# One block of feed-forward, state-space scan and feed-forward on one core: the order of work comes from tables, and TensorE adds matmuls of zeros to y in steps 2, 31 and 39

## The chip, the cores and the metric

The kernel runs on one core of one Trainium2 chip. The metric is device time in microseconds (us) of one execution; the median of 3 runs of the kernel before is 5074.88 us.

## What is computed

The input x is (4, 2048, 512), all float32. Three sub-blocks are added to x in turn; each takes a layer norm (no weights) of what it is given.

```python
# feed-forward (twice, factor 0.5): token mix with the token before, then
r = sigmoid(xr @ W_r.T);  k = square(relu(xk @ W_k.T));  out = r * (k @ W_v.T)
# state-space block (once), E = 1024 channels, N = 16 states
xz = layernorm(x, ln_w, ln_b) @ W_in.T;  xs, z = split(xz)
xc = silu(b_conv + causal_conv4(xs));  dt, B, C = split(xc @ W_xproj.T)
delta = softplus(dt @ W_dt.T + b_dt)
h_t = exp(delta_t * A) * h_(t-1) + delta_t * B_t * xc_t     # for all 1024 x 16 states
y_t = sum_n h_t * C_t + D_skip * xc_t
out = (y * silu(z)) @ W_out.T + x
```

## The kernel before

The 8192 tokens are worked on in 16 **chunks** of 512 tokens, the four batches in turn. A chunk has 64 **steps**: 4 quarters of the channels (256 channels, two tiles of 128) by 16 states. In step s, for the state s % 16 of the quarter s // 16:

- ScalarE (ACT) makes `decay` = exp(delta * A), in two instructions and a one-column copy between them (`make_decay`, L837 to L840), into one of two buffers. It has first to save the last column of the buffer's old content (`save`, L846), which waits for the step before the last to be done.
- GpSimd (POOL) makes `dbx` = u * B (`product`, L1255, and a one-column sum, L1259), up to four steps ahead.
- VectorE (DVE) runs the scan in place (`scan`, L1037, 128x1024) and multiplies by C (`weigh`, L1045) into `g`, of which there are two.
- TensorE (PE) adds g to the accumulator `y_acc` in PSUM by eight 128x128 transposes (`sum_g`, L510), one step later.
- SyncE loads B and C of the next steps, spread over 128 partitions.

Everything else is put between these, at fixed steps of the same loop: feed-forward 0 and the first half of the state-space block of the chunk in front (`front`, chunk it+1), the gate and output of this one, and the output projection and feed-forward 1 of the chunk behind (`back`, it-1). Each engine has its own program, in which every piece of work stands in an `if ... s == ...` after the step's own work, so the place in the program and the order of the `if`s fix what is queued behind what. Engines wait for each other by semaphores, whose counts follow from the order of names in a `Marks` list. An engine can run a step or so ahead of another: the decay of step s is made while DVE scans step s-1.

The pieces that matter here: `ffn_norm` (L642) writes the normalized rows of feed-forward 1 over `rows[1]`, so it waits until `res_scratch<-rows` (L336), the store of the residual that `make_res` (L731) wrote there, has landed. `keep_y` (L819) copies y_acc to SBUF at a quarter's end; the first `sum_g` of the next quarter waits for it. `turn_y` (L522) transposes it, DVE multiplies it with the gate (`gate_y`, L1014). `z` (L462) and `xs` (L452) are the two halves of the input projection, each piece of four 128x512 matmuls (eight records); `gate_tanh` (L826) and `gate_silu` (L1008) take z, `conv_start` (L753), `conv_taps` (L997), `conv_tanh` (L762) and `conv_silu` (L1003) take xs. `dt_proj` (L486) and `softplus` (L788, with a table load before and one after, L796) make delta of a quarter. `xproj` (L474), eight matmuls in steps 49 and 50, and `x_rows` (L771) make dt, B and C of the chunk in front. `ffn_turn` is at L401, `ffn_add` at L1244. All outputs of PE but y_acc go through the two banks of `mm`; `GROUPS` lists them in PE's order with their bank, and `bank_free` makes PE wait until the last content of the bank was read.

Of the kernel before, what the change touches and what calls it, by code (L numbers as in the profile page):

```python
# [5 lines left out]
ALU = mybir.AluOpType  # L6
# [4 lines left out]
P = 128  # L11
# [22 lines left out]
def build(nc, x, mu_r, mu_k, w_r, w_k, w_v, ln_w, ln_b, w_in, w_conv, b_conv, w_x, w_dt, b_dt,  # L34
# [20 lines left out]
    with ExitStack() as ctx:  # L55
# [6 lines left out]
        def sem(name):  # L62
# [45 lines left out]
        zero = sb("zero", [P, 1])  # L108
# [27 lines left out]

        newton = ["guess"] + [f"{q}{i}" for i in range(NEWTON) for q in ("yy", "vyy", "half", "y")]
        f_pe = [Marks(sem("ffn0_pe"), "T0 T1 T2 T3 k0 k1 k2 k3 r0 r1 r2 r3 v0 v1 v2 v3"),
                Marks(sem("ffn1_pe"), "T0 T1 T2 T3 r0 r1 r2 r3 k0 k1 k2 k3 v0 v1 v2 v3")]
        f_act = [Marks(sem("ffn0_act"), "ln0 ln1 ln2 ln3 xn0 xn1 xn2 xn3 lead last pk0 pk1 pk2 pk3 "  # L140
                       "pr0 pr1 pr2 pr3 rel0 sq0 rel1 sq1 rel2 sq2 rel3 sq3 th0 th1 th2 th3"),
                 Marks(sem("ffn1_act"), "ln0 ln1 ln2 ln3 xn0 xn1 xn2 xn3 lead last pr0 pr1 pr2 pr3 "
                       "pk0 pk1 pk2 pk3 th0 th1 th2 th3 rel0 sq0 rel1 sq1 rel2 sq2 rel3 sq3")]
        f_dve = [Marks(sem("ffn0_dve"), "st0 st1 st2 st3 mv0 mv1 mv2 mv3 xk0 xk1 xk2 xk3 xr0 xr1 xr2 xr3 "
                       "g0 g1 g2 g3"),
                 Marks(sem("ffn1_dve"), "st0 st1 st2 st3 mv0 mv1 mv2 mv3 xr0 xr1 xr2 xr3 xk0 xk1 xk2 xk3 "
                       "g0 g1 g2 g3")]
# [22 lines left out]
        y_pe = Marks(sem("y_pe"), "T0 T1 T2 T3 T4 T5 T6 T7 o0 o1 o2 o3")  # L170
        y_dve = Marks(sem("y_dve"), "g0 g1 g2 g3 g4 g5 g6 g7 x0 x1 x2 x3")


        GROUPS = [("f0T0", 1, f_act[0], "xn0", 1), ("f0T1", 1, f_act[0], "xn1", 0),
                  ("f0T2", 1, f_act[0], "xn2", 1), ("f0T3", 1, f_act[0], "xn3", 0),
                  ("YT6", -1, y_dve, "g6", 1), ("YT7", -1, y_dve, "g7", 0), ("dt1_0", 0, h_act, "xa1", 1),
                  ("dt1_1", 0, h_act, "xb1", 0), ("o0", -1, y_dve, "x0", 0), ("f0k0", 1, f_act[0], "rel0", 1),
                  ("f0k1", 1, f_act[0], "rel1", 0), ("f0k2", 1, f_act[0], "rel2", 1),
                  ("f0k3", 1, f_act[0], "rel3", 0), ("f0r0", 1, f_act[0], "th0", 1),
                  ("f0r1", 1, f_act[0], "th1", 0), ("f0r2", 1, f_act[0], "th2", 1),  # L180
                  ("f0r3", 1, f_act[0], "th3", 0), ("f0v0", 1, f_dve[0], "g0", 1),
                  ("f0v1", 1, f_dve[0], "g1", 0), ("f0v2", 1, f_dve[0], "g2", 1),
                  ("f0v3", 1, f_dve[0], "g3", 0), ("dt2_0", 0, h_act, "xa2", 1), ("dt2_1", 0, h_act, "xb2", 0),
                  ("o1", -1, y_dve, "x1", 1), ("o2", -1, y_dve, "x2", 0), ("o3", -1, y_dve, "x3", 1),
                  ("mT0", 1, m_act, "xn0", 0), ("mT1", 1, m_act, "xn1", 1), ("mT2", 1, m_act, "xn2", 0),
                  ("mT3", 1, m_act, "xn3", 1), ("z0", 0, z_dve, "0", 0), ("xs0", 1, m_dve, "c2_0", 1),
                  ("z1", 0, z_dve, "1", 0), ("xs1", 1, m_dve, "c2_1", 1), ("YT0", 0, y_dve, "g0", 0),
                  ("YT1", 0, y_dve, "g1", 0), ("z2", 0, z_dve, "2", 1), ("dt3_0", 0, h_act, "xa3", 0),
                  ("dt3_1", 0, h_act, "xb3", 1), ("xs2", 1, m_dve, "c2_2", 0),
                  ("f1T0", -1, f_act[1], "xn0", 1), ("f1T1", -1, f_act[1], "xn1", 1),  # L190
                  ("f1T2", -1, f_act[1], "xn2", 1), ("f1T3", -1, f_act[1], "xn3", 1),
                  ("xs3", 1, m_dve, "c2_3", 0), ("z3", 0, z_dve, "3", 1), ("xs4", 1, m_dve, "c2_4", 0),
                  ("YT2", 0, y_dve, "g2", 1), ("YT3", 0, y_dve, "g3", 1), ("xs5", 1, m_dve, "c2_5", 0),
                  ("f1r0", -1, f_act[1], "th0", 1), ("f1r1", -1, f_act[1], "th1", 1),
                  ("xs6", 1, m_dve, "c2_6", 0), ("f1r2", -1, f_act[1], "th2", 1),
                  ("f1r3", -1, f_act[1], "th3", 1), ("xs7", 1, m_dve, "c2_7", 0),
                  ("f1k0", -1, f_act[1], "rel0", 1), ("f1k1", -1, f_act[1], "rel1", 0),
                  ("xp", 1, m_act, "xp", 1), ("f1k2", -1, f_act[1], "rel2", 0),
                  ("f1k3", -1, f_act[1], "rel3", 1), ("dt0_0", 1, h_act, "xa0", 0),
                  ("dt0_1", 1, h_act, "xb0", 1), ("f1v0", -1, f_dve[1], "g0", 0),  # L200
                  ("f1v1", -1, f_dve[1], "g1", 1), ("f1v2", -1, f_dve[1], "g2", 0),
                  ("f1v3", -1, f_dve[1], "g3", 1), ("z4", 0, z_dve, "4", 0), ("z5", 0, z_dve, "5", 1),
                  ("z6", 0, z_dve, "6", 0), ("YT4", 0, y_dve, "g4", 1), ("YT5", 0, y_dve, "g5", 1),
                  ("z7", 0, z_dve, "7", 0)]
# [1118 lines left out]
```

## Time and profile before

| | us |
|---|---|
| median of 3 runs (lowest, highest) | 5074.88 (5071.17, 5075.77) |
| the profiled execution's own time | 5075.57 |
| its span, first to last instruction | 5073.8 |
| PE busy | 4318.3 (85%) |
| DVE busy | 4484.9 (88%) |
| ACT busy | 2897.2 (57%) |
| POOL busy | 3179.3 (63%) |

The profile is of one execution. Its views are: a page (busy times, and the span in 40 slices with TensorE's granted clock), the waits (who waited for whom in total), busy times in stretches of the span, and the timeline (instructions in order of time, merged; in brackets the idle time of the engine before one and what ended it). Matmul records overlap, since matmuls are pipelined.

### The profile page before, as it was taken

What the parts mean: (1) busy time and instruction counts of PE and PEld (TensorE: products, weight loads), DVE (VectorE), ACT (ScalarE), POOL (GpSimd) and SP (SyncE); (2) the same over time, 40 slices, a digit from 0 to 9 for tenths busy, and PEclk for the clock granted to TensorE, in tenths of its full rate; (3) what the DMA queues carried; (4) which work ended last, traced back from release to release, by engine and by line L of the source; (5) the groups of instructions that cost most, each with busy time, mean ns of one, the idle gap of its engine ahead of it and who ended that gap; (6) DMA issues with size and microseconds to landing.
All of it is one profiled execution on the core that took longest, in us unless ns stands there. A gap on an engine that the chain in (4) does not pass through costs nothing.

```text
span 5073.8 us, 57587 instructions
## 1 busy us (share of the span) xinstructions
PE 4318.3 (85%) x16640; PEld 2420.2 (48%) x16640; DVE 4484.9 (88%) x3650; ACT 2897.2 (57%) x6355; POOL 3179.3 (63%) x3328
## 2 busy tenths in 40 slices
PE   6778889898888989889898888989889898888777
PEld 2444445454454545445454454545445454454443
DVE  2799999899999999899899999999899899998982
ACT  3555656566565656656565655656656566565552
POOL 1666667576675756667576665756667576675761
PEclk9888999899999999999999999989999999999788
DMA  2445656465654656556565655656566565654651
GB/s 79 146 138 176 164 168 181 137 180 152 181 166 147 182 165 173 162 167 183 143 179 147 183 165 151 179 168 170 165 174 171 150 179 144 179 166 138 172 156 63
DMA packets 423052, 810.69 MB, mean 160 GB/s; under 512 B 41264, under 2 KB 41264, under 8 KB 418640
## 3 DMA queue, kind: packets, MB, share of 16 engines
q1 hardware_dynamic: 422736, 807.00, 55.4%
q8 instruction: 135, 2.21, 0.2%
q14 instruction: 181, 1.48, 0.1%
HBM read 772.25 MB, written 34.60 MB: 159 GB/s over the span
## 4 chain that ended last, share of the span: by engine, by line
PE 39%; DVE 24%; issue 12%; ACT 9%; POOL 8%; DMA 6%; SPq 0%; DVEq 0%; POOLq 0%; ACTq 0%
DVE decay L1037 10%; PE y_acc L510 9%; DVE g L1045 8%; PE mm L437 6%; POOL dbx L1255 5%; PE mm L415 5%; PE mm L426 5%; PE mm L462 4%; PE mm L452 4%; DMA res_scratch<-rows 3%; DMA c_all<-bc_scratch 3%; DVE xc L997 3%; PE mm L474 3%; PE mm L486 1%; DVE mix_k L974 1%
## 5 line engine op out<-in xcount | busy, mean ns | idle before, releaser
L1255 POOL TENSOR_TENSOR dbx<-u,b_all 128x1024 f32<-128x1024 f32 x1024 | 2413.3, 2357 | 1211.0 <-DVE g L1045 1207.9
L1037 DVE TENSOR_TENSOR_SCAN decay<-decay,state,dbx 128x1024 f32<-128x1024 f32 x1024 | 2405.9, 2350 | 261.2 <-ACT decay L840 253.4
L510 PE MATMUL y_acc<-ident,g 128*128 128x128 f32 x8192 | 1177.9, 291 | 541.3 <-DVE g L1045 472.1
L510 PEld LDWEIGHTS y_acc<-ident,g 128*128 128x128 f32 x8192 | 992.1, 149 | 1092.0 <-DVE g L1045 766.2
L1045 DVE TENSOR_TENSOR g<-decay,c_all 128x1024 f32<-128x1024 f32 x1024 | 1242.0, 1213 | 7.9 <-DMA c_all<-bc_scratch 0.9
L837 ACT ACTIVATE decay<-delta,neg_a 128x512 f32<-128x512 f32 x1024 | 708.6, 692 | 36.9
L840 ACT ACTIVATE decay<-delta,neg_a 128x511 f32<-128x511 f32 x1024 | 686.8, 671 | 0.0
L437 PE MATMUL mm<-wbuf_c,col 128*128 128x512 f32 x1024 | 460.8, 594 | 21.9 <-ACT delta L788 20.5
L846 ACT ACTIVATE state<-decay 128x2 f32<-128x2 f32 x1024 | 167.3, 163 | 454.8 <-DVE g L1045 453.8
L997 DVE SCALAR_TENSOR_TENSOR xc<-mm,conv_sb,xc 128x509 f32<-128x509 f32 (+2 forms) x384 | 285.1, 743 | 64.3 <-ACT xs_last L755 55.0
L1259 POOL TENSOR_TENSOR dbx<-dbx,carry 128x1 f32<-128x1 f32 x1024 | 247.1, 241 | 80.3
L437 PEld LDWEIGHTS mm<-wbuf_c,col 128*128 128x128 f32 x1024 | 185.1, 190 | 212.6 <-issue 210.4
L452 PE MATMUL mm<-xn_col,wbuf_a 128*128 128x512 f32 x512 | 257.8, 652 | 1.4 <-DVE xc L997 1.4
L753 ACT ACTIVATE xc<-mm,evec,conv_sb 128x512 f32<-128x512 f32 x128 | 99.2, 775 | 276.1 <-PE mm L452 241.9
L462 PE MATMUL mm<-xn_col,wbuf_c 128*128 128x512 f32 x512 | 254.9, 645 | 0.0
L707 ACT ACTIVATE col<-mm 128x512 f32<-128x512 f32 x128 | 76.8, 600 | 299.2 <-PE mm L415 299.2
L452 PE MATMUL mm<-xn_col,wbuf_d 128*128 128x512 f32 x512 | 239.8, 612 | 1.2 <-ACT xn_col L740 0.9
L415 PE MATMUL mm<-mix_k,wbuf_c 128*128 128x512 f32 x512 | 234.8, 603 | 4.4 <-DVE mix_k L974 4.4
L826 ACT ACTIVATE gate<-mm 128x512 f32<-128x512 f32 x128 | 76.2, 595 | 284.1 <-PE mm L462 284.0
L426 PE MATMUL mm<-wbuf_d,xin 128*128 128x512 f32 x512 | 233.4, 600 | 4.4 <-DVE xin L979 4.4
L533 PE MATMUL mm<-wbuf_a,gate 128*128 128x512 f32 x512 | 234.0, 600 | 2.1 <-DVE gate L1014 0.8
L462 PE MATMUL mm<-xn_col,wbuf_b 128*128 128x512 f32 x512 | 231.7, 595 | 0.0
(98 smaller groups left out, 5170.0 us busy)
## 6 DMA issues: line engine op xcount, KB each, us to landing
b_all<-bc_scratch SPq DMA_DIRECT2D x1024, 256.0 KB, 3.9
c_all<-bc_scratch SPq DMA_DIRECT2D x1024, 256.0 KB, 4.6
wbuf_d<-in_w_r SPq DMA_DIRECT2D x32, 1024.0 KB, 8.6
wbuf_c<-in_w_v SPq DMA_DIRECT2D x32, 1024.0 KB, 8.1
xin<-in_x SPq DMA_DIRECT2D x16, 1024.0 KB, 8.1
wbuf_c<-in_w_k SPq DMA_DIRECT2D x16, 1024.0 KB, 8.2
wbuf_d<-in_w_in SPq DMA_DIRECT2D x16, 1024.0 KB, 8.0
wbuf_a<-in_w_in SPq DMA_DIRECT2D x16, 1024.0 KB, 9.8
```

Of the source, the lines that this page charges most:

```text
L415: last = pe.matmul(bank(it, f"f{i}k{j}"), wk[:, ct, j * P:(j + 1) * P], mix_k[:, ct, :], start=ct == 0, stop=ct == CT - 1)
L426: last = pe.matmul(bank(it, f"f{i}r{tb}"), mix_r[:, ct, tb * P:(tb + 1) * P], wr[:, ct, :], start=ct == 0, stop=ct == CT - 1)
L437: last = pe.matmul(bank(it, f"f{i}v{tb}"), col[:, ct, tb * P:(tb + 1) * P], wv[:, ct, :], start=ct == 0, stop=ct == CT - 1)
L452: last = pe.matmul(bank(it, f"xs{e}"), win[:, ct, e % 4 * P:(e % 4 + 1) * P], xn_col[:, slot, ct, :], start=ct == 0, stop=ct == CT - 1)
L462: last = pe.matmul(bank(it, f"z{e}"), win[:, ct, e % 4 * P:(e % 4 + 1) * P], xn_col[:, slot, ct, :], start=ct == 0, stop=ct == CT - 1)
L510: last = pe.matmul(y_acc[:, tb, j * P:(j + 1) * P], g[:, s % PAIRS, j, tb * P:(tb + 1) * P], ident[:, :], start=n == 0 and j == 0 and tb % ...
L837: act.activation(d[:, 0, :], delta[:, q % 2, 0, :], ACT.Exp, scale=neg_a[:, e, n:n + 1]).then_inc(decay_done, 1)
L840: act.activation(d[:, 1, 1:W], delta[:, q % 2, 1, 1:W], ACT.Exp, scale=neg_a[:, e + 1, n:n + 1]).then_inc(decay_done, 1)
L997: dve.scalar_tensor_tensor(out=o, in0=src[:, 0:W - late], scalar=conv_sb[:, e, q:q + 1], in1=o, op0=ALU.mult, op1=ALU.add).then_inc(m_dve. ...
L1037: dve.tensor_tensor_scan(d, d, flat(dbx[:, s % DBX, :, :]), state[:, batch, s, 0:1], ALU.mult, ALU.add).then_inc(scan_done, 1)
L1045: dve.tensor_tensor(g[:, s % PAIRS, :, :], decay[:, s % PAIRS, :, :], c_all[:, s % CRING, :].unsqueeze(1).broadcast_to([P, QT, W]), ALU.mu ...
L1255: pool.tensor_tensor(dbx[:, s % DBX, :, :], u[:, q % 2, :, :], b_all[:, s % BRING, :].unsqueeze(1).broadcast_to([P, QT, W]), ALU.mult).the ...
```

## The change

The order is now written as tables of step numbers, one for each kind of work, and each engine's program asks the tables in one fixed order. A number below 0 or above 63 means the iteration before or after. Names in `Marks` lists and `GROUPS` are sorted from the tables. Of the tables two lines, with the new one:

```diff
-                    if back and 19 <= s < 25:
-                        out_proj(it, b, (s - 17) // 2, (s - 19) % 2)
+        OUT = ((4, 5), (19, 20), (21, 22), (23, 23))
...
+        RES = 25
...
+        ZEROS = {2: 2, 31: 2, 39: 2}
```

```diff
-        zero = sb("zero", [P, 1])
+        zero = sb("zero", [P, P])
...
-            pe.wait_ge(init_pool, 3)
+            pe.wait_ge(init_pool, 12)
...
+            def add_zeros(n):
+
+                for _ in range(n):
+                    pe.matmul(flat(y_acc[:, 0:2, :]), zero[:, :], ident[:, :].unsqueeze(1).broadcast_to([P, 4, P]),
+                              start=False, stop=False, skip_group_check=True)
...
+                    if scn and s in ZEROS:
+                        add_zeros(ZEROS[s])
...
-                    if front and s == 27:
-                        make_res(f)
-                    if back and s == 30:
-                        ffn_norm(1, b, front)
...
+                    if front and s == RES:
+                        make_res(f)
+                    if back and s == NORM[1]:
+                        ffn_norm(1, b, front)
```

`add_zeros` comes last in its step: two matmuls of a zero 128x128 tile with 512 columns, added to y_acc, so y does not change. It is called three times in each of the 16 chunks: 96 such matmuls in all.

The tables hold most numbers of before, but not all. Moved to another step:

- ACT: `make_res` 27 to 25; `skip_columns` of the four quarters 56, 12, 29, 41 to 58, 14, 31, 43; `ffn_before_r` of feed-forward 0 from 5, 6, 6, 6 to 6, 7, 7, 7.
- PE: the first `ffn_k` of feed-forward 0 from 6 to 5; the last part of `out_proj` 24 to 23.
- DVE: the third gate of feed-forward 0 from 17 to 18, the last `out_stats` 26 to 27, one `ffn_mix_r` of feed-forward 1 from 38 to 39.
- POOL: the four `ffn_add` of feed-forward 1 from 59, 60, 61, 62 to 57, 58, 59, 60.
- SyncE: the load of w_k for feed-forward 1 from 26 to 25, the second load of w_in 27 to 26, the store of the residual 28 to 26, the store of the output 63 to 61.

Four `mamba_turn` outputs and the third `ffn_turn` of feed-forward 1 (from bank 1 to bank 0) changed banks. And within a step the order of some pieces is another, on ACT, PE and DVE.

**ACT, steps 24 to 30** of a chunk, where the residual (`rows<-xin`, the second such row) and the norm of feed-forward 1 (`rows<-xout`) stand. Before, from after step 26's decay:

```order
L740 ACTIVATE xn_col<-mm,vec 128x512 x2
L846 ACTIVATE state<-decay 128x2
...
L740 ACTIVATE xn_col<-mm,vec 128x512 x2
L731 ACTIVATE rows<-xin,shift,rs 128x512 x4
...
L642 ACTIVATE rows<-xout,shift,rs 128x512 x4
L826 ACTIVATE gate<-mm 128x512
L762 ACTIVATE rows<-xc 128x512
```

Now, from step 25:

```order
L781 ACTIVATE rows<-xin,shift,rs 128x512 x4
L896 ACTIVATE state<-decay 128x2
...
L790 ACTIVATE xn_col<-mm,vec 128x512 x2
...
L876 ACTIVATE gate<-mm 128x512
L812 ACTIVATE rows<-xc 128x512
L692 ACTIVATE rows<-xout,shift,rs 128x512 x4
```

The residual is made before the columns of `mamba_columns`, not after them, and the gate's and the convolution's tanh now stand ahead of the norm.

**ACT, step 49**, `keep_y` of quarter 2 (`y_rows<-y_acc`) beside relu and square of feed-forward 1 (`col`). Before:

```order
L707 ACTIVATE col<-mm 128x512
L709 ACTIVATE col<-col 128x512
L819 ACTIVATE y_rows<-y_acc 128x512 x2
L846 ACTIVATE state<-decay 128x2
```

Now:

```order
L869 ACTIVATE y_rows<-y_acc 128x512 x2
L757 ACTIVATE col<-mm 128x512
L759 ACTIVATE col<-col 128x512
L896 ACTIVATE state<-decay 128x2
```

`keep_y` no longer stands behind the relu, which waits for four matmuls; in step 33 it moved ahead of the gate's tanh in the same way.

**PE, steps 31 to 33**: the transposes of y, the third z, the projection of dt for quarter 3. Before:

```order
L522 MATMUL mm<-ident,y_rows 128x128 x8
L510 MATMUL y_acc<-ident,g 128x128 x8
L462 MATMUL mm<-xn_col,wbuf_c 128x512 x4
L510 MATMUL y_acc<-ident,g 128x128 x8
L486 MATMUL mm<-xdbl,wdt_sb 128x512
L494 MATMUL y_acc<-ident,spare 128x128 x8
L486 MATMUL mm<-xdbl,wdt_sb 128x512
```

Now:

```order
L586 MATMUL mm<-ident,y_rows 128x128 x8
L576 MATMUL y_acc<-ident,zero 128x512 x2
L568 MATMUL y_acc<-ident,g 128x128 x8
L520 MATMUL mm<-xn_col,wbuf_c 128x512 x4
L568 MATMUL y_acc<-ident,g 128x128 x8
L544 MATMUL mm<-xdbl,wdt_sb 128x512 x2
L552 MATMUL y_acc<-ident,spare 128x128 x8
```

The zeros stand behind the transposes of y and ahead of `sum_g`, and both dt matmuls now come before the skip terms.

## Rows read from the trace of the kernel before

**Rows 1.** Span with the mean granted clock, and the page's clock in 40 slices.

```profile
core 0: 5073.8 us, clock 0.935
...
PEclk9888999899999999999999999989999999999788
```

**Rows 2.** The waits: who waited for whom, us in total, times, longest us.

```profile
ACT rows L642 <- DMA res_scratch<-rows: 56.9, 14, 5.2
...
DVE decay L1037 <- ACT decay L840: 253.4, 187, 20.1
...
ACT xdbl L771 <- PE mm L474: 126.2, 16, 8.1
```

**Rows 3.** Stretches: from:to length, busy PE, PEld, DVE, ACT, POOL, PEclk, DMA, GB/s.

```profile
3183.99:3487.75 303.76, 266.43 (x1040) 148.91 (x1040) 280.10 (x230) 180.64 (x397) 198.43 (x207) 0.95 0.58 166
3184.00:3193.10 9.10, 5.85 (x48) 5.18 (x48) 9.03 (x6) 8.35 (x21) 6.90 (x5) 1.00 0.75 242
3312.40:3337.90 25.50, 17.12 (x58) 10.42 (x59) 19.16 (x17) 12.81 (x28) 11.20 (x12) 0.73 0.46 133
```

**Rows 4.** Timeline, steps 27 to 30 (start, us, instruction, idle time before it).

```profile
3298.31 2.92 ACT L731 ACTIVATE rows<-xin,shift,rs 128x512 f32<-128x512 f32 x4
...
3303.95 0.38 SPq L336 DMA_DIRECT2D res_scratch<-rows  x1
...
3313.17 0.20 POOL L1227 TENSOR_TENSOR xc<-xc,head 128x3 f32<-128x3 f32 x1
...
3315.19 2.93 ACT L642 ACTIVATE rows<-xout,shift,rs 128x512 f32<-128x512 f32 x4 [3.60 <-DMA res_scratch<-rows]
3318.02 0.57 ACT L826 ACTIVATE gate<-mm 128x512 f32<-128x512 f32 x1
...
3319.92 0.67 ACT L840 ACTIVATE decay<-delta,neg_a 128x511 f32<-128x511 f32 x1
```

**Rows 5.** Timeline of PE, steps 32 and 33.

```profile
3327.46 1.97 PE L510 MATMUL y_acc<-ident,g 128*128 128x128 f32 x8 [2.18 <-DVE g L1045]
3329.22 5.52 PE L462 MATMUL mm<-xn_col,wbuf_c 128*128 128x512 f32 x8
```

**Rows 6.** Timeline of DVE, steps 33 to 35.

```profile
3335.41 0.69 DVE L1008 SCALAR_TENSOR_TENSOR gate<-gate,mm 128x512 f32<-128x512 f32 x1 [1.76 <-ACT gate L826]
...
3344.36 2.36 DVE L1037 TENSOR_TENSOR_SCAN decay<-decay,state,dbx 128x1024 f32<-128x1024 f32 x1 [2.30 <-ACT decay L840]
```

**Rows 7.** Timeline of PE and DVE, steps 36 and 37.

```profile
3350.31 1.08 PE L401 MATMUL mm<-ident,rows 128*128 128x128 f32 x4 [0.78 <-ACT col L659]
...
3352.90 3.94 PE L452 MATMUL mm<-xn_col,wbuf_d 128*128 128x512 f32 x8
...
3357.74 1.53 DVE L997 SCALAR_TENSOR_TENSOR xc<-mm,conv_sb,xc 128x509 f32<-128x509 f32 x2 [1.43 <-ACT xs_last L755]
```

**Rows 8.** Timeline of PE and DVE, steps 49 to 52.

```profile
3421.34 1.48 PE L510 MATMUL y_acc<-ident,g 128*128 128x128 f32 x8 [2.42 <-ACT y_rows L819]
3422.75 4.87 PE L474 MATMUL mm<-xc,wx_sb 128*64 128x512 f32 x8
...
3428.58 3.65 PE L474 MATMUL mm<-xc,wx_sb 128*64 128x512 f32 x8
...
3434.53 2.36 DVE L1037 TENSOR_TENSOR_SCAN decay<-decay,state,dbx 128x1024 f32<-128x1024 f32 x1 [4.17 <-ACT decay L840]
```

**Rows 9.** Timeline of POOL, DVE and ACT, steps 55 to 58.

```profile
3449.80 2.37 POOL L1255 TENSOR_TENSOR dbx<-u,b_all 128x1024 f32<-128x1024 f32 x1
...
3453.03 0.65 DVE L986 SCALAR_TENSOR_TENSOR rows<-rows,mm 128x512 f32<-128x512 f32 x1
...
3460.37 2.92 ACT L642 ACTIVATE rows<-xin,shift,rs 128x512 f32<-128x512 f32 x4
```

**Rows 10.** Timeline of PE, steps 2 and 3.

```profile
3195.75 1.24 PE L510 MATMUL y_acc<-ident,g 128*128 128x128 f32 x8 [2.61 <-DVE g L1045]
3196.78 3.47 PE L486 MATMUL mm<-xdbl,wdt_sb 128*128 128x512 f32 x4
```

More of the change, by code:

```diff
@@ L169, in build @@
         y_act = Marks(sem("y_act"), "a0 b0 a1 b1 a2 b2 a3 b3")
[L170 to L204, printed above, removed]
@@ L604, in body @@
-                    if scn and s == 51:
-                        sum_skip(it, 3)
-                    if front and s == 53:
+                    if front:
+                        for n in at(TURN[0], s):
+                            ffn_turn(it, 0, f, n)
+                    if scn:
+                        for e in at(YTURN, s):
+                            turn_y(it, it, e)
+                    if back:
+                        for e in at(YTURN, s + 64):
+                            turn_y(it, b, e)
@@ new lines, in body @@
+                    if back:
+                        for n in range(TB):
+                            for part in at(OUT[n], s):
+                                out_proj(it, b, n, part)
+                    if front:
+                        for n in at(MM_K[0], s):
+                            ffn_k(it, 0, f, n)
+                        for n in at(MM_R[0], s):
+                            ffn_r(it, 0, f, n, xn_col[:, other, :, :])
+                        for n in at(MM_V[0], s):
+                            ffn_v(it, 0, f, n)
+                        for n in at(MTURN, s):
+                            mamba_turn(it, f, n)
@@ new lines, in body @@
+                    if scn:
+                        for e in at(Z, s):
+                            z(it, it, e, slot)
+                    if back:
+                        for e in at(Z, s + 64):
+                            z(it, b, e, other)
+                    if front:
+                        for e in at(XS, s):
+                            xs(it, f, e, other)
+                    if back:
+                        for n in at(TURN[1], s):
+                            ffn_turn(it, 1, b, n)
+                        for n in at(MM_R[1], s):
+                            ffn_r(it, 1, b, n, xin)
+                        for n in at(MM_K[1], s):
+                            ffn_k(it, 1, b, n)
@@ L619, in _ @@
+                    if front:
+                        for part in at(XPROJ, s):
+                            xproj(it, f, part)
+                    if back:
+                        for n in at(MM_V[1], s):
+                            ffn_v(it, 1, b, n)
+                    if scn and s in ZEROS:
+                        add_zeros(ZEROS[s])
             run(body, pe)
@@ L939, in body @@
-                    if front and s == 51:
-                        x_rows(f)
-                    if front and s == 54:
+                    if scn:
+                        for q in at(KEEP_Y, s):
+                            keep_y(it, q)
+                    if back:
+                        for q in at(KEEP_Y, s + 64):
+                            keep_y(b, q)
+                    if front:
+                        for n in at(COLUMNS[0], s):
+                            ffn_columns(0, f, n)
+                            if n == CT - 1:
+                                ffn_lead(0, f, fb)
@@ new lines, in body @@
+                    if back:
+                        for n in at(COLUMNS[1], s):
+                            ffn_columns(1, b, n, front)
+                            if n == CT - 1:
+                                ffn_lead(1, b, bb)
+                    if front:
+                        for n in at(MCOLS, s):
+                            mamba_columns(f, n, other)
+                        for n in at(RELU[0], s):
+                            ffn_relu2(0, f, n)
+                        for n in at(TANH[0], s):
+                            ffn_tanh(0, f, n)
@@ new lines, in body @@
+                    if back:
+                        for n in at(RELU[1], s):
+                            ffn_relu2(1, b, n)
+                        for n in at(TANH[1], s):
+                            ffn_tanh(1, b, n)
+                    if scn:
+                        for e in at(GATE_TANH, s):
+                            gate_tanh(it, e)
+                    if back:
+                        for e in at(GATE_TANH, s + 64):
+                            gate_tanh(b, e)
+                    if front:
+                        for e in at(TAP0, s):
+                            conv_start(f, e, fb)
+                        if s == XROWS:
+                            x_rows(f)
@@ L942, in body @@
+                    if front and s == DELTA[0] + 64:
                         softplus(f, 0, 0)
@@ L1118, in body @@
+                    if back and s == MEANS[1]:
+                        row_means(1, f_dve[1], b)
                     if scn:
```

502 lines of the change are left out of this document (237 added, 265 removed), and 3 rows, old and new, of the table BANK.

## The prediction

> **What bounds the kernel now.** I read the page first. Its line of TensorE's clock [rows 1] shows a mean granted clock of 0.935 and a pattern that repeats by chunk. Since the levels are 1.2 and 2.4 GHz, 0.935 means that 13% of the span, (1 - 0.935) x 2 x 5073.8 = 660 us, is at the lower one. Next comes a middle chunk from end to end (first of [rows 3]): 303.76 us, in which DVE is busy for 280.10, PE for 266.43, POOL for 198.43, ACT for 180.64. So DVE is the engine that the rest has to feed, and what it stands still, 303.76 - 280.10 = 23.7 us in a chunk, is most of what a new order can win without shortening any work. One step costs DVE no less than a scan and a product, 3.5 us, and a mean step takes 303.76 / 64 = 4.75.
>
> Then the waits in total [rows 2]: DVE waits for ACT's decay for 253.4 us, ACT for the landing of the residual's store for 56.9 us in 14 chunks, ACT for PE's dt, B and C rows for 126.2 us in 16. The timeline tells where these stand, in the chunk from 3183.99 on, and each of the places below is one of them. The lower clock matters where PE is what others wait for. Steps 31 to 33 (third of [rows 3]) have a mean clock of 0.73, and there the third z takes 5.52 us [rows 5], against 3.65 for eight 128x512 records at the full clock ([rows 8], the second xproj row, of a smaller tile but as many columns).
>
> I call 0.2%, 10 us, what a measurement of this kernel can tell from no change.
>
> **The change, part by part**, per chunk.
>
> *A, the residual, step 30.* ACT's norm waits 3.60 us for the store [rows 4], 56.9 / 14 = 4.06 in the mean [rows 2]. The store was issued at 3303.95 and the wait ended at 3315.19, 11.2 us later. `make_res` and the store are two steps earlier now, 7 us at 3.5 a step, so the store lands ahead of 3311.6, where ACT began to wait. Next late is what now stands ahead of the norm: the convolution's tanh needs POOL's head sum, done at 3313.17 + 0.20 = 3313.37. With tanh 0.62 and the norm's 2.93 ACT comes to the next `save` at 3316.9; before, it came there after 3318.50 + 0.62 = 3319.1, hence 2.1 us earlier. To this 4.06 - 3.60 = 0.46 for the mean: 2.5. DVE had its scan of this step behind it, so decay is what ends the wait, and all of it shows. Bounds 0 and 4.06.
>
> *C1, the clock, step 33.* `sum_g` of step 32 ran at the lower clock (1.97 us) after PE had stood idle for 2.18, and the third z behind it took 5.52 [rows 5]. DVE waits 1.76 us for the gate's tanh on that z [rows 6]. The zeros of one step are two matmuls of 512 columns, four records, as many as the two dt matmuls. Those took 3.47 at the lower clock [rows 10], and half of the eight records of xproj at the full clock is 1.8 [rows 8]: so the zeros take 1.8 or 3.5. In step 31 they fill the idle 2.18. If the clock is high when z starts, z is done 1.9 earlier and DVE's 1.76 go. I take 1.7. Bounds 0 and 1.76.
>
> *C2, steps 34 and 35.* DVE waits 2.30 us for a decay [rows 6] that stands behind the softplus of quarter 3. Softplus needs both dt projections, and these now run ahead of the skip terms, behind a z that is done earlier. `keep_y` also comes before the gate's tanh, so PE goes on 0.6 sooner. 1.9; bounds 0 and 2.30.
>
> *D, steps 36 and 37.* The third `ffn_turn` ran at the lower clock and the xs behind it took 3.94 [rows 7]; DVE waits 1.43 us. With the other bank that piece doesn't wait in line with its neighbours, and xs starts earlier. 1.4; bounds 0 and 1.43.
>
> *E, steps 49 to 52.* `sum_g` waits 2.42 us for `keep_y` [rows 8], which stands behind a relu. Without that gap xproj starts 2.4 earlier, and its first piece may do without 4.87 - 3.65 = 1.2 of low clock: `x_rows` come 3.6 earlier. ACT waits 126.2 / 16 = 7.9 us there [rows 2], and DVE stands 4.17 behind it [rows 8]. I take 3.5, as little else is queued. Bounds 0 and 4.17.
>
> *F, step 3.* dt at the lower clock takes 3.47 [rows 10]. Zeros in step 2 fit in PE's idle 2.61 at the full clock. 0.3; bounds 0 and 0.6.
>
> *G, POOL, step 57.* `ffn_add` of feed-forward 1 comes two steps earlier. It needs the gate that DVE makes at 3453.03 + 0.65, while POOL is free to start at 3449.80 [rows 9]. POOL waits 3453.68 - 3449.80 = 3.9 us, with `dbx` of coming steps and the rsqrt chain queued behind. ACT's norm of 2.92 us at 3460.37 [rows 9] comes later by what its slack, 2.1 by my reading, doesn't cover. `dbx` is up to four steps ahead, which covers most. The skip columns of quarter 0 (two instructions of 128x512, some 0.7 each like those of [rows 4]) that left step 56 give 1.4 back. -0.7; bounds -3.9 and 0.
>
> *H, the rest.* Zeros that start at the lower clock take 3.5 in a gap of 2.2: 1.3 late, once or not at all. The zeros of step 39 stand in a like gap, and the clock may fall in new places. -0.3; bounds -1.8 and 0. PE's longer wait at the start costs nothing, since PE has first to wait for data. The `skip_columns` two steps later, the moved mixes and loads have steps of slack: 0.
>
> **Sum**: 2.5 + 1.7 + 1.9 + 1.4 + 3.5 + 0.3 - 0.7 - 0.3 = 10.3 us for each of the 14 chunks that have one in front and one behind, 144, and 5 for the two ends, which have only part of it: 149. From the profiled execution's 5075.57 this gives 4926; the median stands 0.7 lower, which is nothing here. All upper bounds together are 14.3 a chunk, 4876.
>
> **A rule against the sum.** Between 3184.00 and 3193.10 PE ran only transposes, 5.85 us busy in 9.10, and its granted clock was 1.00 (second of [rows 3]). The low clock in steps 31 to 33 came behind idle time [rows 5]. So the transposes themselves did not bring it down. The Trainium skill, "TensorE: Matmul & The Clock Gate", Part 4, says that transposes in PE mode don't count as PE being busy in the same way and that the full clock doesn't engage for them. By it, true matmuls of zeros among transposes would do more than filling a gap does, and the low stretches elsewhere, with transposes alone in them, would stay.
>
> **Rivals.**
> *R2: the clock stays down in steps 31 to 33.* Zeros in step 31 alone may not lift it before z, as 3 gaps of 2 to 3.5 us lie in a row there. For it: the stretch began in step 30, ahead of the zeros. Against: A takes 2.1 out of the first gap. Then C1 (1.7) and half of C2 (1.0) are lost, and the zeros take the 1.3 of H: 10.3 - 3.6 = 6.7, 94 + 4, **4977**.
> *R3: the wins are given back.* The order is nearly the same, and what ends one wait can be replaced by another in line: norm by head sum, x_rows by the next thing in step 52 (its skip sums now precede a projection). For it: ACT has several pieces in every such step. If A and E give half and C1 to D half, (6.0 + 5.0) / 2 - 1.0 = 4.5 a chunk, 63 + 2: **5010**.
> *R4: time at the low clock is all lost time.* The rows say that a piece at the lower clock takes up to twice as long; if all of the 660 us counted and half of it came back, 5076 - 330 = **4746**. Against it: DVE's 280.10 of 303.76 leave no more than 23.7 a chunk. The Trainium skill, the same page, Terms, puts the penalty at the throttled time by one minus the clock's share, which is this reckoning; the row on DVE speaks against it.
> *R5: slower, by POOL.* G's wait of 3.9 shows in full, as POOL's cover of four steps is used up where the rsqrt chain stands. It decides if the other terms together give under 3.9 a chunk: with A alone (2.5), -1.4 x 14 = -20, **5095**. Against it: D and E don't hang on the clock.
> *R6: nothing.* The tables only rename, and DVE's own work bounds: **5075**. Against it, the moves above are real in the list of instructions.
>
> **Chances.** Forecast 0.70, R2 0.15, R3 0.08, R4 0.02, R5 0.02, R6 0.03. The range of the forecast itself is from all upper bounds, 4876, to about two thirds of the sum, 4975; R2 lies at its end. I give 4872 to 4990, which leaves out R3 to R6 and a little of the rest. Faster 0.95, same 0.03, slower 0.02.
>
> **What would show it.** A: the wait for the store gone. C1: the third z at 3.6. C2: DVE's wait for decays from 253.4 to about 120. E: `keep_y` not waited for 2.4, x_rows waits about 4.4. The mean clock at 0.97 or more, the chunk at 293.5, POOL waiting 3.9 before `ffn_add` in step 57. It is wrong if the wait for the store is gone but the chunk is not 2 us shorter in step 30, if z stays at 5.5, or if DVE's wait in step 52 stays over 3.

## The result, and the profile after

| | before | after |
|---|---|---|
| median of the runs (lowest, highest) | 5074.70 (5071.17, 5075.77) | 4942.70 (4941.35, 4949.61) |
| span of the profiled execution | 5073.8 | 4947.8 |
| mean granted clock | 0.935 | 0.958 |
| DVE busy | 4484.9 (88%) | 4493.3 (91%) |

The ratio is 0.9744, with a 95% interval of 0.9727 to 0.9761: 132 us less in the medians, where 149 were forecast (4926), and inside the range. All times are in us. Every ratio is taken against runs of the kernel before on the same chip; differences in us between two changed kernels are of medians that can be from different chips, on which the kernel before itself had medians from 5071.1 to 5075.3.

The waits of the kernel after, beside [rows 2]. The wait of ACT's norm for the store of the residual is not among them any more.

```profile
DVE decay L1086 <- ACT decay L890: 195.2, 161, 19.9
...
POOL xout L1282 <- DVE rows L1021: 109.2, 19, 46.9
...
ACT xdbl L821 <- PE mm L532: 73.5, 16, 7.9
```

DVE waits 58 us less for decay, ACT 53 us less for PE's dt, B and C. DVE's wait for decay was to fall to about 120, and is 195.2: see the signs in the part on the prediction. One wait is new: POOL's for the gate (before: 53.6 in 4 times, now 109.2 in 19).

One chunk of the kernel after, as a stretch, beside [rows 3]; columns as there.

```profile
2808.60:3103.90 295.30, 265.46 (x1052) 146.72 (x1052) 280.43 (x229) 181.01 (x397) 200.32 (x207) 0.98 0.58 171
```

A chunk takes 295.30 in place of 303.76 and DVE works as long as before, so it now stands still for 14.9 and not 23.7. The chunk that was forecast is 293.5.

To find where it went I took the time from each scan's start to the next one's on DVE, which is the length of a step, as the mean over chunks 1 to 14, and subtracted. The profiled execution of the changed kernel is the slowest of its four, 7 us above their median, so lengths of its steps are if anything a little long (`none` marks steps for which the forecast had no term):

| steps | term | forecast | before to after, a chunk |
|---|---|---|---|
| 29 to 31 | A | -2.5 | -3.2 (step 30: 8.76 to 5.72) |
| 33 | C1 | -1.7 | -1.3 (6.10 to 4.84) |
| 34 | C2 | -1.9 | -1.9 (6.41 to 4.46) |
| 36 to 38 | D | -1.4 | -2.2 (37: 7.42 to 6.23) |
| 49 to 53 | E | -3.5 | -3.7 (51: 8.23 to 4.66) |
| 3 to 6 | F | -0.3 | -0.1 |
| 58 to 63 | G | +0.7 | +1.9 (59: 3.98 to 5.33) |
| 39 to 41 | H | +0.3 | +0.9 (39: 6.20 to 7.04) |
| 14 | none | 0 | +1.2 (4.31 to 5.53) |
| 16 to 19 | none | 0 | -0.6 (17: 4.90 to 3.97) |
| all 64 steps | | -10.3 | -9.2 (303.9 to 294.7) |

Step 30 in the timeline of POOL and ACT, beside [rows 4]:

```profile
2938.11 0.19 POOL L1265 TENSOR_TENSOR xc<-xc,head 128x3 f32<-128x3 f32 x1
...
2938.33 0.63 ACT L812 ACTIVATE rows<-xc 128x512 f32<-128x512 f32 x1 [0.87 <-POOL xc L1265]
2938.87 2.91 ACT L692 ACTIVATE rows<-xout,shift,rs 128x512 f32<-128x512 f32 x4
2941.69 0.15 ACT L896 ACTIVATE state<-decay 128x2 f32<-128x2 f32 x1
```

The tanh waits 0.87 for POOL's head sum, and the norm behind it for nothing. PE in steps 31 to 33, beside [rows 5]:

```profile
2946.45 0.63 PE L586 MATMUL mm<-ident,y_rows 128*128 128x128 f32 x4 [3.04 <-DVE gate L1049]
2946.92 2.99 PE L576 MATMUL y_acc<-ident,zero 128*128 128x512 f32 x4
2949.72 1.68 PE L568 MATMUL y_acc<-ident,g 128*128 128x128 f32 x8
2951.24 3.60 PE L520 MATMUL mm<-xn_col,wbuf_c 128*128 128x512 f32 x8
```

The four records of zeros ran partly at the lower clock (2.99, between the 1.8 and 3.5 of the forecast). The third z behind them takes 3.60 in place of 5.52.

PE in step 49, beside [rows 8]: the wait for `keep_y` is gone, and the first xproj takes 3.65 in place of 4.87.

```profile
3037.46 1.09 PE L568 MATMUL y_acc<-ident,g 128*128 128x128 f32 x8 [0.29 <-DVE g L1094]
3038.48 3.65 PE L532 MATMUL mm<-xc,wx_sb 128*64 128x512 f32 x8
```

Where time was lost. First POOL, DVE and SyncE in steps 54 to 59, beside [rows 9]:

```profile
3064.11 0.23 POOL L1276 TENSOR_TENSOR carry<-carry,state 128x16 f32<-128x16 f32 x1
3068.01 1.27 POOL L1282 TENSOR_TENSOR xout<-xout,rows 128x512 f32<-128x512 f32 x1 [3.67 <-DVE rows L1021]
3069.24 2.35 POOL L1293 TENSOR_TENSOR dbx<-u,b_all 128x1024 f32<-128x1024 f32 x1
...
3080.78 0.32 SPq L329 DMA_DIRECT2D b_all<-bc_scratch  x1
3081.21 0.37 SPq L339 DMA_DIRECT2D c_all<-bc_scratch  x1
...
3085.75 1.22 DVE L1094 TENSOR_TENSOR g<-decay,c_all 128x1024 f32<-128x1024 f32 x1 [1.39 <-issue]
```

The first `ffn_add` waits 3.67 for the gate, and `dbx` stands behind it. The load of B waits for its buffer, which POOL's `dbx` frees, and the load of C is queued behind that of B on SyncE. This C was issued at 3081.21 and landed 4.5 later, at 3085.7; DVE's multiplication by C began at 3085.75, after 1.39 idle. The profile shows no releaser for this idle time ("issue"): it is the landing that tells.

Then ACT and DVE in step 14, where `skip_columns` of quarter 1 now stands:

```profile
2870.46 0.60 ACT L763 ACTIVATE rows<-mm 128x512 f32<-128x512 f32 x1 [2.23 <-PE mm L484]
2870.95 1.32 ACT L858 ACTIVATE spare<-xc,evec 128x512 f32<-128x512 f32 x2
2872.18 0.16 ACT L896 ACTIVATE state<-decay 128x2 f32<-128x2 f32 x1
...
2873.86 2.36 DVE L1086 TENSOR_TENSOR_SCAN decay<-decay,state,dbx 128x1024 f32<-128x1024 f32 x1 [1.91 <-ACT decay L890]
```

The 1.32 lie between a tanh that waits for PE and the decay that DVE waits for: DVE waits 1.91, and 0.69 one step before.

And DVE in step 39, with the moved `ffn_mix_r` (L1014) in a step in which DVE never stands still, so that all of it adds to the step:

```profile
2983.80 2.34 DVE L1086 TENSOR_TENSOR_SCAN decay<-decay,state,dbx 128x1024 f32<-128x1024 f32 x1
2986.06 0.92 DVE L1014 SCALAR_TENSOR_TENSOR xin<-col,vec,xin 128x512 f32<-128x512 f32 x1
2986.90 0.67 DVE L1049 TENSOR_TENSOR gate<-gate,mm 128x512 f32<-128x512 f32 x1
2987.50 2.30 DVE L1032 SCALAR_TENSOR_TENSOR xc<-mm,conv_sb,xc 128x509 f32<-128x509 f32 x3
2989.72 1.21 DVE L1094 TENSOR_TENSOR g<-decay,c_all 128x1024 f32<-128x1024 f32 x1
```

### The profile page after: what moved, and what is told of

Same layout as the page of the kernel before. It is cut to its first block, busy times and chain, and to the rows that moved or that the text cites. A ratio compares the mean times of both kernels' runs of the same rounds, so it can differ in the third digit from the quotient of the medians.

```text
span 4947.8 us, 57971 instructions
## 1 busy us (share of the span) xinstructions
PE 4318.2 (87%) x16832; PEld 2400.0 (49%) x16832; DVE 4493.3 (91%) x3650; ACT 2902.5 (59%) x6355; POOL 3206.1 (65%) x3328
## 4 chain that ended last, share of the span: by engine, by line
DVE 34%; PE 20%; issue 18%; POOL 16%; ACT 6%; DMA 4%; DVEq 0%; SPq 0%; POOLq 0%; ACTq 0%
DVE decay L1086 16%; POOL dbx L1293 10%; DVE g L1094 10%; PE mm L484 5%; DMA c_all<-bc_scratch 4%; PE y_acc L568 4%; DVE xc L1032 3%; PE mm L473 3%; PE mm L532 2%; PE mm L495 2%; POOL xout L1282 1%; DVE xc L1038 1%; PE mm L510 1%; PE mm L520 1%; ACT rows L692 1%
## 5 line engine op out<-in xcount | busy, mean ns | idle before, releaser
L1086 DVE TENSOR_TENSOR_SCAN decay<-decay,state,dbx 128x1024 f32<-128x1024 f32 x1024 | 2406.0, 2350 | 198.7 <-ACT decay L890 195.2
L568 PE MATMUL y_acc<-ident,g 128*128 128x128 f32 x8192 | 1139.5, 285 | 368.3 <-DVE g L1094 363.7
L568 PEld LDWEIGHTS y_acc<-ident,g 128*128 128x128 f32 x8192 | 961.5, 146 | 945.1 <-DVE g L1094 729.1
L1297 POOL TENSOR_TENSOR dbx<-dbx,carry 128x1 f32<-128x1 f32 x1024 | 274.0, 268 | 80.3
L763 ACT ACTIVATE rows<-mm 128x512 f32<-128x512 f32 x128 | 76.6, 598 | 319.1 <-PE mm L484 319.1
L510 PE MATMUL mm<-xn_col,wbuf_a 128*128 128x512 f32 x512 | 233.0, 599 | 1.4 <-DVE xc L1032 1.4
L520 PE MATMUL mm<-xn_col,wbuf_c 128*128 128x512 f32 x512 | 231.4, 595 | 0.8 <-ACT xn_col L790 0.8
```

What stands on the lines that cost most here:

```text
L510: last = pe.matmul(bank(it, f"xs{e}"), win[:, ct, e % 4 * P:(e % 4 + 1) * P], xn_col[:, slot, ct, :], start=ct == 0, stop=ct == CT - 1)
L520: last = pe.matmul(bank(it, f"z{e}"), win[:, ct, e % 4 * P:(e % 4 + 1) * P], xn_col[:, slot, ct, :], start=ct == 0, stop=ct == CT - 1)
L568: last = pe.matmul(y_acc[:, tb, j * P:(j + 1) * P], g[:, s % PAIRS, j, tb * P:(tb + 1) * P], ident[:, :], start=n == 0 and j == 0 and tb % ...
L1086: dve.tensor_tensor_scan(d, d, flat(dbx[:, s % DBX, :, :]), state[:, batch, s, 0:1], ALU.mult, ALU.add).then_inc(scan_done, 1)
```

## The experiments

All but one start from the changed kernel. Numbers in brackets behind a ratio are its 95% interval; the changed kernel itself has 0.9744 [0.9727, 0.9761].

**1. The zeros.**

```diff
-        ZEROS = {2: 2, 31: 2, 39: 2}
+        ZEROS = {}
```

> The changed kernel with ZEROS empty; the order is kept. Theory 1 (zeros lift the clock for steps 32 to 36, and cost 1 us a chunk in steps 39 and 40): step 33 goes back by 1.5 us, 34 by part of its 2.2, step 3 or 4 by 0.5, and 39 gives 1.0 back: 1.5 to 3 us a chunk longer, 4965 to 4985, third z at 5.5, clock about 0.94. Theory 2 (the order alone did it, zeros only cost): the clock is low, but nobody waits for it, 1 us a chunk shorter, about 4928.

Measured: 4981.13, ratio 0.9816 [0.9799, 0.9834], 38 us slower than with them. PE:

```profile
2966.20 1.97 PE L568 MATMUL y_acc<-ident,g 128*128 128x128 f32 x8 [2.63 <-DVE g L1094]
2967.96 5.02 PE L520 MATMUL mm<-xn_col,wbuf_c 128*128 128x512 f32 x8
```

Steps 33, 34 and 4 are longer by 0.69, 1.09 and 0.29, all in all 2.0 a chunk. Theory 1 holds, but for its last clause: step 39 gives nothing back, it stays at 7.04. So with the new order in place the zeros account for 2.0 of the 9.2 a chunk between before and after. How much is theirs depends on what else is there, as run 2 shows.

**2. The zeros alone, in the kernel before**, with `add_zeros` and the zero tile of the change.

```diff
+                    if scn and s in (2, 31, 39):
+                        add_zeros(2)
```

> The kernel before with the zeros at the ends of steps 2, 31 and 39 and nothing else. Theory 1 (the zeros lift the clock wherever they stand): third z at 3.6, steps 33, 34 and 4 shorter by 1.8, 0 to 1 and 0.5, step 39 longer by 0.8: 1.5 to 2.5 a chunk, 5040 to 5055. Theory 2 (without the earlier residual the clock has fallen in step 30 and stays down, the zeros run at half speed): 1 us a chunk longer, about 5090.

Measured: 5023.26, ratio 0.9898 [0.9882, 0.9914]: 51 us faster, more than either theory had. Theory 1 named the place rightly, but not the size, and step 39, which it had longer by 0.8, stays at 6.20.

```profile
2980.93 1.97 PE L516 MATMUL y_acc<-ident,g 128*128 128x128 f32 x8 [3.66 <-DVE g L1053]
...
2985.09 1.88 PE L502 MATMUL y_acc<-ident,zero 128*128 128x512 f32 x4
...
2988.82 3.60 PE L462 MATMUL mm<-xn_col,wbuf_c 128*128 128x512 f32 x8
```

The clock still falls at the end of step 30, as before, and is high again by the time of the zeros, which take 1.88. What had a price at the lower clock gets shorter all over the chunk: step 33 by 1.00, 36 and 37 by 1.50, 51 by 0.43, 4 and 5 by 0.32, 34 by 0.20. So the zeros and the order share some of their gain: zeros are worth 51 us on the old order and 38 on the new.

**3. No zeros in step 39.**

```diff
-        ZEROS = {2: 2, 31: 2, 39: 2}
+        ZEROS = {2: 2, 31: 2}
```

> The changed kernel without the zeros of step 39. Theory 1 (those zeros end after g is ready and hold up sum_g, and buy nothing): step 39 at 6.2 and 40 at 5.9 as before, 1.0 us a chunk, 4928. Theory 2 (they hold the clock up for steps 41 and on, or the 0.84 comes from the order of work in step 39): 4940 or above.

Measured: 4948.88, ratio 0.975 [0.9734, 0.9765], not told apart from the change. Step 39 stays at 7.04 and 40 at 6.09: theory 1 falls. These zeros neither cost nor buy anything, though they end after g is ready. The mean granted clock fell from 0.958 to 0.955 without them, and the time did not follow. The 0.84 of step 39 is the mix (runs 11 and 12).

**4. The adds back.**

```diff
-        FFN_ADD = ((19, 20, 21, 22), (57, 58, 59, 60))
+        FFN_ADD = ((19, 20, 21, 22), (59, 60, 61, 62))
```

and the output's store in step 63.

> The changed kernel with ffn_add of feed-forward 1 in steps 59 to 62 again and the output's store in 63. Theory 1 (the earlier adds push POOL's dbx back, so the buffer of B comes free later, SyncE issues B and behind it C later, and DVE waits for C in step 59): steps 58, 59 and 61 shorter by 0.25, 1.3 and 0.15, 1.7 a chunk, 4918. Theory 2 (DVE's wait in step 59 comes from the other moves): 4938 to 4945.

Measured: 4928.75, ratio 0.9712 [0.9697, 0.9727], 14 us faster than the change. Steps 58, 59 and 61 are shorter by 0.26, 1.35 and 0.17, as expected, and POOL goes from u straight to `dbx`:

```profile
3047.17 2.35 POOL L1271 TENSOR_TENSOR u<-delta,xc 128x1024 f32<-128x1024 f32 x1
3049.48 0.22 POOL L1276 TENSOR_TENSOR carry<-carry,state 128x16 f32<-128x16 f32 x1
3049.66 2.35 POOL L1293 TENSOR_TENSOR dbx<-u,b_all 128x1024 f32<-128x1024 f32 x1
```

It falls short of 4918, since step 37 came out 0.80 longer in the mean. That step has two lengths, 5.7 and 7.0, and a chunk takes the longer one where the clock is low in step 36: in 6 of the 14 chunks of the change, and in all 14 of this run. The same two pieces of PE in a short chunk of the change and in a long one:

```profile
2673.77 1.04 PE L568 MATMUL y_acc<-ident,g 128*128 128x128 f32 x8
2674.65 3.60 PE L510 MATMUL mm<-xn_col,wbuf_d 128*128 128x512 f32 x8
...
2969.05 1.91 PE L568 MATMUL y_acc<-ident,g 128*128 128x128 f32 x8
2970.76 3.94 PE L510 MATMUL mm<-xn_col,wbuf_d 128*128 128x512 f32 x8
```

The count of long chunks moves from run to run, also where an edit is far from step 36: 2 in run 8, 5 in run 10, 7 in run 3.

**5. The residual back in place.**

```diff
-        RES = 25
+        RES = 27
```

and its store in 28 (`"res_out": 28`).

> The changed kernel with make_res in step 27 and the store of the residual in step 28 again; the tanh pieces stay ahead of the norm. Theory 1 (term A, the store's landing held the norm): ACT waits for res_scratch again, 3 to 4 us a chunk; the gate's and the convolution's tanh, 1.2 us, now lie inside that wait, so step 30 is longer by about 2 and not 3: 4965 to 4980. Theory 2 (it was the order of the tanh pieces alone): step 30 stays under 6, 4943.

Measured: 4937.16, ratio 0.9735 [0.9718, 0.9751]. There is no wait for the store, and step 30 is 5.27, shorter than in the change. Theory 1 falls: the moves of `make_res` and its store, on which term A rested, are not needed. They do not even help: with `make_res` in it, step 27 is 0.66 longer, and 29 and 30 are shorter by 0.23 and 0.44, which is nothing in all; run 5 and the change are not told apart. Why, runs 6 and 7 tell.

**6. The loads back too.** As 5, and w_k and the second half of w_in in steps 26 and 27 (now 25 and 26).

> The changed kernel with make_res in 27 and the store in 28 (as in res_back), and w_k and the second half of w_in loaded in steps 26 and 27 again, so that 2 MB stand close ahead of the store. Theory 1 (in res_back the store landed in 8.3 us instead of 10 to 11 because the loads had a step's lead; ACT now asks for it 9.9 after its issue, no longer 7.7, since the tanh pieces come first): landing 10 to 11, a wait of about 1 us for it returns, step 30 at 6.3, 4950. Theory 2 (the loads don't matter, the order of the tanh pieces alone hides the landing): no wait, 4937.

Measured: 4973.3, ratio 0.9797 [0.9783, 0.9812]. The waits:

```profile
ACT rows L692 <- DMA res_scratch<-rows: 19.4, 14, 2.3
```

1.4 us a chunk, step 30 at 6.77. The store is issued in the same step as in run 5, but two loads of 1 MB each stand closer ahead of it: the median from issue to landing is 9.1, the longest 12.2, where run 5 had 8.3 and 9.1. Theory 1 holds in its mechanism. Its 4950 was far too low: the run is 31 us slower than the change. The steps account for 1.43 a chunk, 20 us; this run's profiled execution, 4961.72, was the fastest of its four by 11 us, and what the others lost beside it is not shown.

**7. The norm ahead of the tanh pieces too.** As 6, with

```diff
+                    if back and s == NORM[1]:
+                        ffn_norm(1, b, front)
                     if scn:
                         for e in at(GATE_TANH, s):
...
-                    if back and s == NORM[1]:
-                        ffn_norm(1, b, front)
```

> As res_loads_back, and the norm ahead of the gate's and the convolution's tanh in step 30 again: all of term A undone, by residual, loads, store and order. Theory 1 (the order was the part that mattered, as ACT comes to the norm 2 us earlier when it is first): the wait for the residual's store is back at 3 to 5 us a chunk, step 30 at about 8.7, 3 us a chunk: 4985. Theory 2 (what matters is that skip_columns left step 29 or that xout is ready earlier): the wait stays under 1, 4940 to 4950.

Measured: 4980.06, ratio 0.9812 [0.9797, 0.9826].

```profile
ACT rows L692 <- DMA res_scratch<-rows: 76.5, 14, 6.0
```

5.5 us a chunk, more than the 4.06 of before, and step 30 at 7.81. Theory 1 holds in kind: the wait is back, though step 30 is 7.81 and not 8.7. The change has three covers for the landing: two steps' lead of the store, the loads out of its way, and the tanh pieces ahead of the norm. The last two are enough (run 5); the tanh pieces alone leave 1.4 of 5.5 (run 6); what the lead alone would hide was not run. Between 6 and 7, step 30 grows by 1.04 and 31 by 0.31, while 34 and 37, whose lengths the clock moves, shrink by 0.21 and 0.35: 0.75 a chunk, 10 us, and 7 in the medians, which by their intervals are not told apart.

**8. keep_y behind relu in step 49.**

```diff
-                    if scn:
+                    if scn and s != 49:
                         for q in at(KEEP_Y, s):
                             keep_y(it, q)
...
                         for n in at(RELU[1], s):
                             ffn_relu2(1, b, n)
+                    if scn and s == 49:
+                        keep_y(it, 2)
```

> The changed kernel with keep_y behind relu and square of feed-forward 1 in step 49 again, all else kept. Theory 1 (term E, PE's gap for keep_y makes xproj and x_rows late): PE's gap of 2.4 is back, step 51 goes from 4.66 to about 7.8, step 49 +0.17: 3.3 a chunk, 4990. Theory 2 (the skip terms ahead of ffn_k in step 51 and the full clock made most of it): step 51 under 6, 4950 to 4965.

Measured: 4983.65, ratio 0.9827 [0.9812, 0.9841], 41 us slower.

```profile
3056.46 1.06 PE L568 MATMUL y_acc<-ident,g 128*128 128x128 f32 x8 [2.41 <-ACT y_rows L869]
...
3068.00 2.36 DVE L1089 TENSOR_TENSOR_SCAN decay<-decay,state,dbx 128x1024 f32<-128x1024 f32 x1 [2.51 <-ACT decay L890]
```

PE's gap of 2.41 is back, step 51 is 7.73 (+3.07). Theory 1 holds. Two instructions in another order are the largest single part of the change that was taken back.

**9. The banks back.**

```diff
-        "mT": (1, 0, 1, 0)
+        "mT": (0, 1, 0, 1)
...
-        "f1T": (1, 1, 0, 1)
+        "f1T": (1, 1, 1, 1)
```

> The changed kernel with the four mamba_turn outputs and the third ffn_turn of feed-forward 1 in their old banks. Theory 1 (term D, the shared bank made that piece wait): steps 36 to 38 longer by 1.4, 4963. Theory 2 (D came from the clock and from the order of mix and silu in step 38): within 0.3 us a chunk, 4940 to 4947, and PE's four turns in step 35 to 36 wait no longer than now.

Measured: 4976.5, ratio 0.981 [0.9795, 0.9824], 34 us slower. The turns in step 35 and 36 wait one after the other again:

```profile
2979.50 0.63 PE L459 MATMUL mm<-ident,rows 128*128 128x128 f32 x4 [0.78 <-ACT col L709]
2980.91 0.63 PE L459 MATMUL mm<-ident,rows 128*128 128x128 f32 x4 [0.78 <-ACT col L709]
```

Steps 36 and 37 are longer by 1.31 and 0.90: 2.2 a chunk. The steps of the `mamba_turn` outputs, 25 and 26, keep their lengths, so it is the third `ffn_turn` that counts. Theory 1 holds, at more than the 1.4 that it expected.

**10. The skip columns back.**

```diff
-        SKIP = (-6, 14, 31, 43)
+        SKIP = (-8, 12, 29, 41)
```

> The changed kernel with skip_columns in steps 56, 12, 29 and 41 again. Theory 1 (in step 14 ACT has no slack, its decay waits behind tanh and 1.4 us of skip columns; in 12 it has): step 14 from 5.53 to 4.31, others within 0.3: 1.2 a chunk, 4926. Theory 2 (they only move: step 12, 29 or 41 grows by as much): 4940 to 4950.

Measured: 4932.69, ratio 0.9724 [0.9709, 0.9738]. Step 14 is shorter by 1.66 and 13 by 0.78, 12 longer by 1.22, and 16, 18 and 19 by 0.65 in all: -0.6 a chunk. Neither theory is right as stated: in step 12 the two instructions cost as much as in 14, but the steps behind it catch up.

**11. What costs, undone together**, and **12. with one more matmul of zeros** between the second and the third `ffn_turn` of step 35. Run 11 is 4 and 5 together, `SKIP = (-6, 12, 31, 43)`, the mix of step 39 in 38, no zeros in 39; run 12 adds

```diff
                             ffn_turn(it, 1, b, n)
+                            if n == 1:
+                                add_zeros(1)
```

> What the runs so far found to cost, undone together: ffn_add in 59 to 62 and the output's store in 63 (-1.8 a chunk), skip_columns of quarter 1 in step 12 (-0.6), ffn_mix_r of step 39 in 38 (I expect 38 at 5.3 and 39 at 6.2, -0.4), make_res and the store in 27 and 28 (-0.3), no zeros in 39 (0). If these add, 3.1 a chunk: 4943 - 43 = 4900. Rival: step 39's 0.84 is the new place of mix_r relative to other work and stays, and step 37 goes to 7 in every chunk as in add_back (clock low in 36): 4920.

> As best1, with one more matmul of zeros between the second and third ffn_turn in step 35, where PE stands idle 1.7 us. Theory 1 (the clock falls in step 36 because of the idle time in 35): low clock in 36 gone, step 37 at 5.68 in all chunks, 0.6 to 1.3 a chunk under best1: 4888. Theory 2 (those 0.9 us don't keep it up, or delay the turns): as best1 or 5 to 10 us more.

Measured: 4911.27, ratio 0.9678 [0.9664, 0.9693], and 4904.26, ratio 0.9667 [0.9651, 0.9683]. Both are faster than the change, by their intervals and by some 31 and 38 us in the medians, and not told apart from each other by their intervals. Step 39 goes to 6.19 and 38 to 5.49: the mix costs 0.85 in 39 and 0.66 in 38, a net 0.2 and not the 0.4 expected. Step 37 is 6.40 in run 11 and 5.89 in run 12. In run 11 the clock is low in step 36 in 7 of 14 chunks, with step 37 at 6.9 to 7.4 there; in run 12 it is low there in none, and step 37 is between 5.7 and 6.0 in every chunk. So theory 1 has the mechanism, and not the size: the short steps became up to 0.3 longer, and the chunk is 0.3 shorter where 0.6 to 1.3 were expected. As the count of low chunks moves by itself from 2 to 14 over the runs, none in one profiled execution is strong evidence, not proof. PE in steps 35 to 37 of a chunk of run 12:

```profile
2934.55 0.59 PE L576 MATMUL y_acc<-ident,zero 128*128 128x512 f32 x1
2934.98 1.04 PE L459 MATMUL mm<-ident,rows 128*128 128x128 f32 x8
2935.85 1.04 PE L568 MATMUL y_acc<-ident,g 128*128 128x128 f32 x8
2936.72 3.60 PE L510 MATMUL mm<-xn_col,wbuf_d 128*128 128x512 f32 x8
```

## Why the prediction was right, and where its steps were not

The forecast of 149 us came out as 132. The sum was near, and most places were the right ones; one mechanism was put on the wrong move, and three costs were too small. That the sum came so near is in part luck: by the table, the steps of terms A to F gave 12.4 for the 11.3 forecast and others 0.6, while the costs were 4.0 for 1.0, and the two errors took away from each other. The 5 us for the two ends did not come in the profiled executions: 9.2 x 14 = 129, and the spans differ by 126.

- **A**: the place and the size (3.2 for 2.5) were right, the cause was not. "`make_res` and the store are two steps earlier now ... so the store lands ahead of 3311.6, where ACT began to wait" is true of the trace, but run 5 takes the two steps away and no wait comes back. What the text called "next late", the tanh pieces that now stand ahead of the norm, is itself a cover, as is the earlier load (runs 6, 7). The step that failed is the one from "two steps earlier" to "the store lands ahead" as the cause of the gain: three moves could each cover the landing, and only one was asked for its worth.
- **C1**: right in place, 1.3 for 1.7. The third z takes 3.60; zeros off, 5.02 (run 1). That the zeros would run at one clock or the other was too simple: they ran across the change (2.99). R2, that the clock stays down, did not come: it rose even where the zeros stood alone in the old order (run 2).
- **C2**: right in size (1.9). On the new order 1.1 of it goes with the zeros, and 0.85 is the order's (6.41 to 5.56, run 1); on the old order the zeros alone gave step 34 only 0.20 (run 2).
- **D**: the bank was a right cause (run 9), but not the only one: on the old order the zeros alone, with the old banks, made steps 36 and 37 shorter by 1.50 (run 2). The sum took DVE's wait in step 37 alone; step 36 became shorter by 0.59 as well, 1.8 in place of 1.4. The 0.47 of step 38 in the table's row is not D's: it is the mix that left that step (see H).
- **E**: right, 3.7 for 3.5, by run 8 with nearly all of it from `keep_y`.
- **F**: 0.1 for 0.3: step 4 gave 0.4, but steps 5 and 6 took 0.3 back.
- **G**: mis-sized, 1.9 for 0.7. The wait was there as worked out (3.67 for 3.9). But "`dbx` is up to four steps ahead, which covers most" counted POOL's own lead alone. Late `dbx` also frees the buffer of B late, and C is queued behind B on SyncE, so DVE waited for a load. This is the price of 1.8, in steps 58, 59 and 61, that run 4 takes back. R5, which let all of it show and the rest fail, did not come.
- **H**: +0.9, and of another cause than "zeros that start at the lower clock" (run 3: nothing). Most of it is the mix, moved from step 38, where DVE had some idle time, to 39, where it had none: +0.84 there and -0.47 in step 38, and a net 0.2 when it is moved back (runs 11 and 12). The text had filed it under "moved mixes and loads have steps of slack: 0". `skip_columns` in step 14 is the second error of that sentence: +1.2, of which steps 16 to 19 gave 0.6 back, and 0.6 net when it is moved back (run 10).
- **The clock**: 0.97 was expected; it is 0.958 in the profiled execution and 0.962 or 0.963 in the three others. Low stretches went on in steps 0, 31, 36 and 39. That in step 36 costs 1.3 where it falls; that in step 39 nothing that runs 1 and 3 could show.
- **R4**, that all low time is lost, gave 4746 and did not come. Beware of the nearest figure: the time at the lower clock, (1 - clock) x 2 x span, fell from 660 to 416, and half of that, 122, is close to the 126 by which the span fell. It is chance, for most of the 126 came by the order of work. Run 2, where the zeros alone differ, decides it: from 660 to 422, half of which is 119, for 51 us measured. In run 1 it is 66 by this reckoning, and 38 measured. That fits low time being lost only where another engine waits for PE.
- **R3**, wins given back to the next wait in line, did not come with its 5010: of gains of 13.0 a chunk 4.0 were given back, not half.
- **The signs**: the wait for the store is gone, z is at 3.60, POOL waits 3.67, x_rows wait 73.5 / 16 = 4.6. One sign missed: DVE's wait for decays was to fall from 253.4 to about 120 and fell to 195.2. The waits that C2 and E named did go, from 2.30 to 0.21 before the scan of step 35 and from 4.20 to 0.64 before that of step 52 (means over chunks 1 to 14). But new ones came: from 0.69 to 1.91 before the scan of step 15, behind the moved `skip_columns`, from 0.25 to 1.66 before that of step 31, and from 1.02 to 1.89 before that of step 53.

By the rule of the Trainium skill, "TensorE: Matmul & The Clock Gate", Part 4, on transposes that don't engage the full clock, the zeros would help because they are true matmuls. The runs agree that zeros lift it; but no run had transposes in the place of the zeros, so whether it is their kind or only that PE was not idle stays open. The stretch of transposes alone at 1.00 in [rows 3] stands against the rule in its strict form.

## What to carry to other kernels

Look for what is queued ahead of a short instruction that another engine waits for: moving one copy ahead of a relu that waits for matmuls was worth 41 us of 132, and a tile in the other PSUM bank 34 (each when taken back alone; such parts overlap and do not add up). When a wait vanishes, ask which of the moves took it, because several may cover the same landing and some of them then only cost. And before a piece is called free at its new step, sum up what the engine does there: a step in which the bounding engine never idles charges the full length, and a late engine also holds back the loads that wait for its buffers.

## What the runs showed of the hardware that was not expected

- Matmuls of zeros in idle time of PE make real matmuls behind them faster: 51 us of 5074 (1.0%) for 96 instructions that compute nothing, although they take 0.59 to 1.06 us a record themselves and their own step may get no shorter. On the better order it was 38.
- The phase of the clock decides single steps: step 37 takes 5.7 or 7.0 from chunk to chunk in one execution, with the same instructions, by whether the lower clock falls on step 36. Mean lengths of that step moved between 5.85 and 7.03 over edits elsewhere, which is up to 1.2 x 14 = 17 us that no edit should be credited with.
- A 1 MB store landed in 8.3 us in the median and 9.1 at most where two loads of 1 MB were issued 10.3 and 5.2 us ahead of it (run 5, one chunk), and in 9.1 and 12.2 where they were 5.2 and 2.2 ahead (run 6).
